# State-space layer of a four-layer decoder: a pipeline over four groups, with the short convolution on VectorE

## What is computed

```python
proj = x @ W_in.T                        # 128 -> z (256), xBC (256 + 64 + 64), dt_raw (2)
conv = depthwise causal conv, 4 taps, over xBC
xBC  = silu(conv + conv_b)
x_ssm, B_ssm, C_ssm = split(xBC)         # 2 heads of 128; 64 states
dt = softplus(dt_raw + dt_bias);  A = -exp(A_log)
# selective scan; with L[q,k] = exp(cs[q] - cs[k]) for k <= q, cs the running sum of dt*A:
y[q] = sum_k (C[q].B[k]) * L[q,k] * dt[k] * x_ssm[k]
y = (y + x_ssm * D_skip) * silu(z)
out = y @ W_out.T
```

## Time and profile before

| what | us |
|---|---|
| median of 3 runs | 1668.62 (1665.03 to 1673.44) |
| the profiled execution's own time | 1673.93 |
| its span | 1671.8 |
| stage L3a within it, from DVE's first step to the next stage's first | 1173.28 to 1341.08 |

### The profile page before, as it was taken

The page is one execution under the profiler, slowest core; times in us unless marked ns, Lnnn a source line. Parts: engine busy times, 40 slices in busy tenths (PEclk is TensorE's granted clock), DMA queues, the critical chain, the costliest instruction groups (busy, mean ns, idle before and its releaser), DMA issues. The chain is left out here.

```text
span 1671.8 us, 30784 instructions
## 1 busy us (share of the span) xinstructions
PE 1253.3 (75%) x9153; PEld 799.4 (48%) x9153; DVE 981.0 (59%) x4171; ACT 639.5 (38%) x1532; POOL 573.1 (34%) x1102
## 2 busy tenths in 40 slices
PE   4799899993482799999945668557778739994786
PEld 2455555542381455555425656456345414543332
DVE  5677777755764777777536635565243338753232
ACT  1356554451131255566522334123232225662221
POOL 3454488872341543544214342243100012210000
PEclk8799999996595699999966977769798958996798
DMA  5435755410112444455001230112000043400000
GB/s 179 140 118 150 219 159 166 148 36 18 44 53 86 141 130 136 149 171 154 27 15 53 66 125 14 35 52 69 15 0 0 0 141 108 124 31 1 0 0 25
DMA packets 139962, 137.80 MB, mean 82 GB/s; under 512 B 12240, under 2 KB 109136, under 8 KB 139552
## 3 DMA queue, kind: packets, MB, share of 16 engines
q1 hardware_dynamic: 131200, 111.40, 21.9%
q0 software_dynamic: 8608, 24.55, 4.6%
HBM read 84.10 MB, written 49.18 MB: 80 GB/s over the span
## 5 line engine op out<-in xcount | busy, mean ns | idle before, releaser
L840 ACT ACTIVATE L0a_Pr<-PS 128x512 f32<-128x512 f32 (+1 forms) x256 | 136.9, 547 | 141.4 <-PE PS L742 89.0
L840 ACT ACTIVATE L1a_Pr<-PS 128x512 f32<-128x512 f32 (+1 forms) x256 | 136.1, 547 | 104.3 <-PE PS L742 51.7
L557 POOL TENSOR_TENSOR L0a_PG<-L0a_Pr,L0a_G 128x512 f32<-128x512 f32 x80 | 105.3, 1320 | 26.6 <-issue 13.0
L963 DVE CUSTOM_DVE_ANT_0 L1a_junk<-PS,L1a_neg 128x256 bf16<-128x256 f32 x256 | 94.8, 420 | 32.1 <-PE PS L715 31.8
L715 PE MATMUL PS<-L0a_Kst,Qm 128*128 128x256 bf16 (+1 forms) x512 | 95.1, 273 | 17.0 <-DVE L0a_mx L963 9.9
L715 PE MATMUL PS<-L1a_Kst,Qm 128*128 128x256 bf16 (+1 forms) x512 | 94.5, 272 | 16.7 <-DVE L1a_mx L963 9.2
L963 DVE CUSTOM_DVE_ANT_0 L1a_junk<-PS,causal_q 128x128 bf16<-128x128 f32 (+1 forms) x256 | 78.5, 353 | 38.1 <-PE PS L715 37.4
L737 PE MATMUL PS<-Qm,L0a_Kst 128*128 128x512 bf16 (+1 forms) x256 | 91.7, 358 | 12.2 <-DMA Qm<-L0a_mT 9.4
L963 DVE CUSTOM_DVE_ANT_0 L0a_junk<-PS,causal_q 128x128 bf16<-128x128 f32 (+1 forms) x256 | 78.5, 352 | 37.1 <-PE PS L715 36.4
L737 PE MATMUL PS<-Qm,L1a_Kst 128*128 128x512 bf16 (+1 forms) x256 | 91.3, 357 | 10.2 <-DMA Qm<-L1a_mT 7.1
L966 DVE TENSOR_REDUCE L3x_mx<-PS 128x2 f32<-128x512 f32 x128 | 84.2, 686 | 23.5 <-PE PS L715 22.9
(11 more groups left out here) (722 smaller groups left out, 3270.8 us busy)
## 6 DMA issues: line engine op xcount, KB each, us to landing
Qm<-q_image SPq DMA_DIRECT2D x160, 128.0 KB
sorted_in<-zeros POOLq DMA_DIRECT2D x16, 516.0 KB, 4.9
L0a_Kst<-k_image SPq DMA_DIRECT2D x64, 128.0 KB
ffn_w_<-L_ffn POOLq DMA_DIRECT2D x32, 256.0 KB, 3.7
L1a_Kst<-k_image SPq DMA_DIRECT2D x64, 128.0 KB
ffn_w_<-L_ffn SPq DMA_DIRECT2D x16, 256.0 KB, 6.9
L3x_Kst<-k_image SPq DMA_DIRECT2D x32, 128.0 KB
k_image<-L0a_kpart SPq DMA_DIRECT2D x16, 192.0 KB
```

The source lines that it names most:

```text
L557: g.tensor_tensor(PG[:, V_ % GATED_RING, :].rearrange("p (h q) -> p h q", h=2), Pr[:, V_ % RING, :].rearrange("p (h q) -> p h q", h=2), G[ ...
L840: a(Pr[:, V_ % RING, 0:2 * nq], PS[:, T_BANK + v % 2, 0:2 * nq], ACT.Exp, scale=SCALE)\
L963: ins = v.tensor_tensor_reduce(junk[:, tt, par, 0:nk], scored[:, par], off, 1.0, LOWEST, ALU.add, ALU.max, mx[:, i % 2, tt, par, hp:hp + 1])
```

## The change

L3a becomes a pipeline over slots, as the attention stages are: 8 slots for a group, no hardware loop, no meeting between groups, and two buffers each for xs, zs and dAb. The projections are made once, without taps: one product of 512 columns for B and C together (128 wide), two for x and two for z. The convolution runs on DVE, from PSUM: for each of the three blocks one `tensor_scalar` with the last tap and three `scalar_tensor_tensor`, each waiting for the one before it, into `acc` in SBUF, from which ACT takes silu with the bias. The layer norm is applied by ACT, half of its scales are computed by POOL; dt is computed in two batches of 8 tiles rather than four of 4; the gating with silu(z) moves from DVE to POOL. The stage's weights, loaded while the stage ahead runs, shrink since the repeated taps are gone. In the attention stages `STACK_IN` becomes (-10, -4).

```diff
-WEIGHTS["L3a"] = [("L3a_z", 2 * P), ("L3a_xs", 2 * P), ("L3a_b", 64), ("L3a_c", 64), ("L3a_dt", 2),
-                  ("L3a_taps_xs", TAPS * 2 * P), ("L3a_taps_b", TAPS * 64), ("L3a_taps_c", TAPS * 64),
+WEIGHTS["L3a"] = [("L3a_z", 2 * P), ("L3a_xs", 2 * P), ("L3a_bc", P), ("L3a_dt", 2), ("L3a_taps", 3 * TAPS), ("L3a_bias", 3),
...
-    STACK_IN, FIRST_STACK_IN = (-13, -7), {"k": -22, "q": -20}
+    STACK_IN, FIRST_STACK_IN = (-10, -4), {"k": -22, "q": -20}
...
+    PER, R = 8, 2
+    G = NPASS
+    BATCH = ((0, 1), (2, 3))
+    SMALL, XS_BANK, BC_BANK, Z_BANK, LA_BANK = 0, 1, 3, 4, 6
+    TURN = {0: -4, 1: -3, 2: 7, 3: 7}
+    STATS, ROOT, NEWTON, APPLY = (-8, -7), (-7, 1), (-6, 1), {0: -5, 1: -4, 2: 6, 3: 6}
+    RAW, ABS, EXP_DT, ONE, LOG_DT, STEP_DT, SUMS, SUMMED = (1, 8), (1, 8), (1, 9), (1, 9), (1, 9), (2, 10), (3, 11), (3, 12)
+    SPREAD, DECAYS, LOGS, EXPS = (lambda g: 3 if g == 0 else PER * g - 4), (lambda g: 4 if g == 0 else PER * g - 2), \
+        (lambda g: 5 if g == 0 else PER * g), (lambda g: 6 if g == 0 else PER * g + 1)
+    PROJECT, CONV, SILU, TURN_X, TURNED_X, MASK, KERNEL = 0, 1, 2, 5, 6, 6, 7
+    TIMES_X, GATE_IN, GATE, OUT, ADD = 10, 12, 13, 14, 15
...
+        def conv(v, step, raw, block):
+            out = two(acc[:, block, :])
+            step(v.tensor_scalar(out, raw, tap(block, TAPS - 1), None, ALU.mult))
+            for j in range(1, TAPS):
+                ins = v.scalar_tensor_tensor(out[:, :, j:], raw[:, :, 0:S - j], tap(block, TAPS - 1 - j), out[:, :, j:],
+                                               ALU.mult, ALU.add)
+                if j < TAPS - 1:
+                    step(ins)
+            return ins
...
-                g.tensor_tensor(Wx[:, :, :], w("L3a_xs").unsqueeze(1).broadcast_to([P, TAPS, NH * P]),
-                                w("L3a_taps_xs").rearrange("p (k c) -> p k c", k=TAPS), ALU.mult).then_inc(s["setup"], 1)
...
+                            g_.tensor_tensor(y3[:, h, :], y2[:, h, :], zs[:, g % R, h, :], ALU.mult).then_inc(s["y3_ready"], 1)
...
-                    for n in range(NH):
-                        for k in range(TAPS):
-                            ins = mm(PS[:, n, :].rearrange("p (b t) -> p b t", b=NSEQ), Wx[:, k, n * P:(n + 1) * P],
-                                     xTp[:, seqs, k:k + S], start=(k == 0), stop=(k == PAD))
...
+                        mm(PS[:, BC_BANK, :], w("L3a_bc"), xT[:, g, :], start=True, stop=True, **free).then_inc(s["bc_psum"], 1)
+                        bank_empty(n, XS_BANK)
+                        mm(PS[:, XS_BANK, :], w("L3a_xs")[:, 0:P], xT[:, g, :], start=True, stop=True, **free).then_inc(s["xs_psum"], 1)
...
+                        for k, rows in enumerate((slice(0, 64), slice(64, P))):
+                            a(BC[:, k, :], acc[rows, NH, :], ACT.Silu, bias=w("L3a_bias")[rows, NH:NH + 1]).then_inc(s["bc_ready"], 1)
```

More of the change, by code:

```diff
@@ L1964, in state_space @@
         sb = core.buffers(c)
[L1965 to L1969, removed]
+        st6, mv = sb("st6", [P, ALL_TILES, 6]), sb("mv", [P, ALL_TILES, 2])
+        var, lnv, r0, nsq, rstd, shift = (sb(n, [P, ALL_TILES]) for n in ("var", "lnv", "r0", "nsq", "rstd", "shift"))
+        xn = sb("xn", [P, ALL_TILES, D])
+        xT = sb("xT", [P, G, NT])
@@ L1970, in state_space @@
+        acc = sb("acc", [P, 3, NT])
+        xs, zs = sb("xs", [P, R, NH, NT]), sb("zs", [P, R, NH, NT])
         BC = sb("BC", [64, 2, NT])
-        zs = sb("zs", [P, NH, NT])
         Xt = sb("Xt", [P, NH, T, P])
         An = sb("An", [P, NH])
[L1974 to L1977, removed]
@@ L1983, in state_space, with group_at @@
-        y2 = sb("y2", [P, NH, NT])
-        y3 = sb("y3", [P, NH, NT])
+        y2, y3 = sb("y2", [P, NH, NT]), sb("y3", [P, NH, NT])
         tri2 = core.W[:, COLS["tri"][0]:COLS["tri"][0] + S]
-        core.n_setup += 4
+        tile = lambda t: core.X[:, t, :]
+        two = lambda ap: ap.rearrange("p (b t) -> p b t", b=NSEQ)
+        tiles_of = lambda k: slice(T * BATCH[k][0], T * (BATCH[k][-1] + 1))
+        tap = lambda block, k: w("L3a_taps")[:, block * TAPS + k:block * TAPS + k + 1]
+        def group_at(n, off):
+            g, r = divmod(n - off, PER)
+            return g if r == 0 and 0 <= g < G else None
@@ new lines, in listed, with planned @@
+        def listed(n, table):
+            return [k for k in range(len(table)) if table[k] == n]
+        def planned(n, slot_of):
+            return next((g for g in range(G) if slot_of(g) == n), None)
+        def conv(v, step, raw, block):
[7 more added lines that the diff above has]
+            return ins
@@ new lines, in newton @@
+        def newton(ops, step, q):
+            step(ops.tensor_tensor(nsq[:, q], r0[:, q], r0[:, q], ALU.mult))
+            step(ops.tensor_tensor(nsq[:, q], nsq[:, q], var[:, q], ALU.mult))
+            step(ops.tensor_scalar(nsq[:, q], nsq[:, q], -0.5, 1.5, ALU.mult, ALU.add))
+            step(ops.tensor_tensor(rstd[:, q], r0[:, q], nsq[:, q], ALU.mult))
+            step(ops.tensor_tensor(shift[:, q], mv[:, q, 0], rstd[:, q], ALU.mult))
+            return ops.tensor_scalar(shift[:, q], shift[:, q], -1.0, None, ALU.mult)
@@ L1992, in _ @@
                 end_pass_sync(core, sp, "state_space")
-                with sp.Fori(0, NPASS) as it:
-                    end_pass_sync(core, sp, "state_space")
                 await_next_weights(core, sp)
@@ L2018, in _ @@
                 free = dict(skip_group_check=True)
[L2019 to L2026, removed]
@@ L2089, in _ @@
                 a = nc.scalar.activation
-                act.wait_ge(s["setup"], core.n_setup)
                 step = Step(act, s["act_step"])
-                act_layernorm(core, act, step, L)
-                for g in range(ALL_TILES // 4):
-                    act.wait_ge(s["xT_psum"], g + 1)
-                    a(xTp[:, g * NSEQ:(g + 1) * NSEQ, PAD:PAD + S], PS[:, g, :].rearrange("p (b t) -> p b t", b=NSEQ),
-                      ACT.Copy).then_inc(s["xT_ready"], 1)
-                end_pass(core, act, "go_act")
@@ L2532, in lay_out @@
     cb = a["L3_attn_conv_b"]
[L2533 to L2538 removed]
+    col["L3a_z"], col["L3a_xs"], col["L3a_bc"], col["L3a_dt"] = (
+        win[:, 0:256], win[:, 256:512], win[:, 512:640], win[:, 640:642])
+    col["L3a_taps"] = taps.reshape(TAPS, 3, P).transpose(2, 1, 0).reshape(P, 3 * TAPS)
+    col["L3a_bias"] = cb.reshape(3, P).T
     col["L3a_alog"], col["L3a_dtb"], col["L3a_skip"] = (
```

463 lines of the change are left out of this document (304 added, 159 removed).

## The result

| what | us |
|---|---|
| changed kernel, median of 4 runs | 1641.97 (1641.02 to 1642.32) |
| kernel before, beside it, 4 runs | 1669.66 |
| ratio | 0.9834, 95% interval 0.9810 to 0.9858 |
| span of the profiled execution | 1639.7, before 1671.8 |

A forecast was written before the change was run, and what follows sets the result against it. It took each L3a group to be bound by one serial chain, no engine being full. L3a falling from 167.8 to 118.5 us saves 49.3, stacks 0, so from the 1668.6 us median the forecast is 1619 us, range 1606 to 1648.

The forecast's parts named there:

- the steady group: L3a, one pipelined group: DVE's work 18.1 us plus 2.2 idle, plus 2.2 for the clock, period 22.5 us.
- the nearest row: L3a convolution on DVE: L2181, one PSUM operand, 0.75 us, was taken as the price basis; 0.78 for all twelve steps.
- the low clock behind PE's quiet stretch: L3a groups: after about 7 us of little PE work, products run at 1.2 GHz, adding 2.2 us a group.
- The way out: L3a after the last group's `Wk`: 8.2 us of steps, 0.8 for low clock, 3.0 for the closing meeting.
- What costs nothing: L3a: POOL's tap folding, the smaller weight load and ACT's extra work, which fits into 22 us, were priced at nothing.
- The way in and group 1: L3a's start: DVE goes on to group 1 at about 39.7 us, and group 1 then takes 22.5 us.
- The sums: L3a's way in: twelve tiny sums on PE at 0.21 us each, moving the reckoning from 23.5 to 26.2 us.
- group 1's idle 2.2: L3a: the second batch's dt steps, 2.3 us, fit into DVE's 2.2 us wait in group 1, adding nothing.
- The stacks: Attention stages: moving the stack loads in SP's queue changes 0 us, ends -1.3 us and the late-stacks rival; slack 5 us.
- What could have made the stacks late: Attention: keys' way out waits for POOL's cut, delaying stacks and scores, 1697 us; with other attention losses, chance 0.05.
- three rivals with a smaller gain: L3a: PE stays at 1.2 GHz (1646 us), shifted steps cost double (1646), groups don't overlap (1640); together 0.26.
- the signs named: L3a about 118 us, steps 0.75, DVE idle 2 to 4, clock 0.8 to 0.95, hole 4; attention within 2 us.

The follow-up runs named there:

- the kernel of the sums: Changed kernel plus an exp-and-log table load ending L3a, with each dt batch's twelve dA-sum products merged into two: 1611.9 us, ratio 0.9675.
- the places: On top of the merged sums, first dt batch's early steps one slot later, second half of layer norm applied one slot earlier: 1612.6 us, ratio 0.9684.

## Why the prediction was right and wrong

**Right in what bounds L3a, and in the steady group.** The group's chain was the thing to read: PE's taps left it, DVE's convolution came to it. The steps cost 0.75 us as the nearest row said. The steady group took 22.6 us against 22.5, with the low clock behind PE's quiet stretch, as 0.50 shows where the earlier trace rows had shown a mix. That it agrees to 0.1 us is in part luck: DVE's work in it was 17.4 us and not 18.1, its two waits 5.2 and not 4.4, and the same code took 21.3 us in the kernel of the sums. Held at the upper level it takes 19.8; 20.3 were worked out. The way out was 12.6 us instead of 12.

**The step that failed most is one that is missing: what state a stage leaves to the next.** "What costs nothing" speaks of ACT's time in a group, but not of which function table ACT holds at the end. The pipeline ends in silu, and L3x has no load of its own: 19 us in L3x, and 17 in the kernel before by the same cause alone. The two programs tell which function is the last in L3a, exp in the one and silu in the other, so the question could have been asked before any run.

**The way in and group 1 were 11 us too short.** The way in took 44.9 us and not 39.7, group 1 took 28.6 and not 22.5. Three terms. The sums were priced at 2.7 us from rows at 2.4 GHz, though PE had idled 10 us ahead of them here. They took 5.1, and some of the decays behind them ran at the lower level too. The second batch's sums were not priced at all, and they stand on PE ahead of the turning for which DVE waits. Its small steps were taken to fall "into group 1's idle 2.2", and they didn't: with the sums merged group 1 still took 25.0 us, with DVE at work for 19.9 and idle for 5.1. And DVE's bias, absolute value and plus one stand ahead of the first convolution, which the sum had behind it: it began at 13.8, not 10.3, of which 1.7 us were left at the end of the small steps. Merging the sums gave 9.2 us back, the places 4.3, and with both L3a takes 116 us against the 118.5 of the forecast.

**The stacks were priced at 0, with -1.3 as the lower end, and gave 6 to 10.** That the maxima were issued at once was true but for one sequence. The step failed in going from there to "not holding them up": with the old place PE waited for the maxima 16 to 19 times in 32, with the new 11 to 14. What could have made the stacks late did not come: the scores waited for `Qm` only at a stage's start.

**The net** of 27.7 us is 38.4 from L3a and about 8 from the stacks, less 19 in L3x; the rest is the spread of stages that did not change. The 1642 us lie within the range of 1606 to 1648, but not where the forecast as worked out put them, 1613 to 1630. They lie where three rivals with a smaller gain had 0.26, and none of the three took place: the shifted steps cost nothing extra, PE did not stay at 1.2 GHz throughout, and the groups overlapped (22.6 us, not 28). So the range held in part by luck: it was wide for other reasons, and the stacks, priced at 0, gave back a part of the unforeseen 19. The same kernel with the old place, for which the prediction gives the same time, took 1652.1 us. Of the signs named, the steps' price, DVE's wait ahead of the masks (3.8 us, released by L2175) and the hole before the second batch (3.3 us) came; L3a's length, the clock of the groups (0.72 to 0.80 instead of 0.8 to 0.95) and the attention stages' length did not.

## What to carry to other kernels

When a stage's order changes, list what it leaves behind for the next one: the function table, the clock, what is in the queues. A chain that is cut by moving work to an idle engine is worth what the chain loses, less what the lower clock takes on the engine that now idles; and many tiny products on the chain cost by their number (twelve took 5.1 us, two in their place 1.0), so merge them before they are moved. That a small transfer is issued at once does not show that the large ones ahead of it in the queue are free: here moving them behind it gave 6 to 10 us, by a mechanism that stays open.

## What was not expected of the hardware

A table load took 1.28 us, and little hid it in L3x, where each of eight layer norms brought one for its log and one for the exp behind it: 20.5 us of loads made the stage 16 to 19 us longer. One silu ahead of a stage that alternates log and exp cost 20 us. Twelve float32 products of two columns took 5.1 us at the lower level of the clock, 0.43 us each, and two of 16 and 8 columns 1.0 us. The same steady group took 22.6 or 21.3 us, by when the clock rose in it. `scalar_tensor_tensor` of 506 to 510 columns from PSUM with a shift of 1 to 3 columns took 0.77 us each with its hop, the same as an unshifted one.
